# Decay exponents of a gated delta-rule kernel: one product of 72 rows from logs summed once, in place of two products with operands made on GpSimd

## The chip, the cores and the metric

The kernel runs on one core of one Trainium2 chip. The metric is the device time in microseconds (us) of one execution. Engines are called as in the profile: PE (TensorE) with its weight loads PEld, DVE (VectorE), ACT (ScalarE), POOL (GpSimd), SP (SyncE, which issues all DMAs here).

## The reference

One block of a transformer: AdaLN modulation, a gated delta-rule attention, then a feed-forward layer with 2:4 sparsity of the hidden activations. Eight sequences of 256 tokens with 256 channels; 16 key heads of 128, two value heads each, so 32 gates. What matters here is the attention:

```python
beta  = sigmoid(x @ W_b.T)                       # (B, T, 32)
dt    = softplus(x @ W_a.T + dt_bias)
decay = exp(-dt * exp(A_log))                    # (B, T, 32)
# per token t, head h, value head p:
Sk = k_t . S;  dv = b_t * (v_t - Sk);  S = S * d_t + outer(k_t, dv);  o = q_t . S
```

The log of the decay, g = -dt * exp(A_log), is what the change is about. In the chunked form of the recurrence each chunk of 128 tokens needs a 128 x 128 matrix of exp(sum of g from token i+1 to token j).

## The kernel before

The tokens are cut into chunks of 128. A step is one key head and two sequences, that is four chunks with two value heads each: U = 8 units of 128 x 128. There are 16 heads times 4 pairs of sequences, 64 steps. They run as a software pipeline, four deep: a body i works on step i (s0: projection, convolution, norms, decays, key products), step i-1 (s1: queries, values, first levels of the triangular inverse, z gate), step i-2 (s2: last levels, residue, state and outputs) and step i-3 (s3: output gate and projection). Each engine has its own list of the parts, written out in `body`, and runs it in that order; the engines meet at semaphores (`need(engine, name, count)`). There is a setup before the first body, two drain bodies (`last_bodies`) after the last, and then the feed-forward layer.

In the setup DVE makes `glog` (128 tokens x 16 chunks x 32 gates) and splits it into two f16 halves, `g_cols`. PE sums the logs along the tokens with the triangles `le`, `lt` and `gt` (three f32 products of 512 columns), and ACT takes the exponentials of these sums for the columns `cols`. For each head `head_columns` copies the head's part to `hg` and `hc`.

In each step POOL makes `g_le` (`decay_operand`, L378): for both halves the mask `le16` times the head's logs, 128 x 1024 f16. PE multiplies it by the mask `gt16` (`decay_product`, two halves h of four units, each half two products of 128x512 that add up in a PSUM bank). ACT then takes the exponentials (`decay_exp`), POOL multiplies by the masked beta (`decay_beta`), DVE by the key products.

The convolution over the tokens has four taps. PE projects block i (keys, queries, two values) into a bank, ACT writes the last tap (`last_tap`, L1096), DVE adds the three others (`convolve`, L1531); the bank is free for projection i+2 when all are done (`bank_project`). The state part of a step goes: PE `first_values`, ACT four scaled copies `us` (in `first_kept`, L1182), PE `state`. SP issues the loads of the next head's weights (`load_weights`, L270), which waits until both halves of the previous ones are made; ACT and DVE split one quarter of them in each step (`split_weights`).

The functions that the diff touches, with line numbers:

Of the kernel before, what the change touches and what calls it, by code (L numbers as in the profile page):

```python
# [35 lines left out]
GUARD = 0.25  # L36
W_SCALE = 64.0
# [8 lines left out]
def adaln_deltanet_ffn(nc, x, wh, nw, wba, dtb, alog, wgate, wup, wdown, cT, wmod, out):  # L46
    with ExitStack() as ctx:  # L47
# [26 lines left out]
        le16 = sb("le16", [P, P], F16)  # L74
        gt16 = sb("gt16", [P, P], F16)
# [11 lines left out]
        g_cols = sb("g_cols", [P, 2, NT, NV], F16)  # L87
# [7 lines left out]
        hg = sb("hg", [P, 2, 2, NT, PV], F16)  # L95
# [11 lines left out]
        g_le = sb("g_le", [P, 2, U, P], F16)  # L107
# [57 lines left out]
        same = hm  # L165
        gate_store = nc.dram_tensor("gate_store", (B, 2 * C), F32, kind="Internal").ap()
# [8 lines left out]
        wu_flat = [g_le[:].rearrange("p r u s -> p (r u s)"), yl[:, 0:2].rearrange("p l u s -> p (l u s)")]  # L175
# [47 lines left out]
        def all_steps(eng, body, last_bodies):  # L223
            for i in range(STEPS + 1):
                body(*lags(i))
            for i in range(STEPS + 1, STEPS + MOST):
                last_bodies(*lags(i)[2:])
# [23 lines left out]
        def _(sp):  # L251
# [13 lines left out]

            def load_weights(head, count):
# [5 lines left out]
            for head in range(1, NK):  # L272
                load_weights(head, head)
# [5 lines left out]
            sp.wait_ge(sig("gate_dma"), 16)  # L279
# [39 lines left out]
        def _(pool):  # L319
# [28 lines left out]
            triangle(le16, ones, ALU.is_ge, 0.0, 1, -1)  # L348
            triangle(gt16, ones, ALU.is_gt, 0.0, -1, 1)
# [22 lines left out]
            def decay_operand(s):  # L372
                n = N(s)
                need(pool, "hc", (head(s) + 1) * 2)
                need(pool, "e_ps", n * 2)
                ts = slice(blk(s) * TL, blk(s) * TL + TL)
                for part in range(2):
                    gp.tensor_tensor(g_le[:, part], le16[:].unsqueeze(1).broadcast_to([P, U, P]),  # L378
                                     hg[:, par(s), part, ts].rearrange("p t v -> p (t v)").unsqueeze(2)
                                     .broadcast_to([P, U, P]), ALU.mult).then_inc(sig("g_le"), 1)  # L380
# [7 lines left out]
            def masked_beta(s):  # L388

                n = N(s)  # L390
                need(pool, "hc", (head(s) + 1) * 2)
# [80 lines left out]
            def body(s0, s1, s2, s3):  # L472
                if s3:
                    gate_output(s3)
                if s1:
                    first_inverse(s1)
                if s0:
                    decay_operand(s0)
# [3 lines left out]
                if s1:  # L482
                    low_half(s1)
# [5 lines left out]
            def last_bodies(s2, s3):  # L489

# [4 lines left out]
                else:  # L495
# [9 lines left out]
                else:  # L505
# [17 lines left out]
        def _(pe):  # L523
# [52 lines left out]
            pe.wait_ge(sig("g_log"), 1)  # L576
            pe.wait_ge(sig("same_ready"), NL)
            pe.wait_ge(sig("pool_const"), 13)
# [7 lines left out]
            pe.wait_ge(sig("cum_exp"), 1)  # L586
            pe.wait_ge(sig("ba_copied"), 2)

# [15 lines left out]
            def decay_product(h, s):  # L604
                need(pe, "g_le", N(s) * 2 + 2)
                us_ = slice(4 * h, 4 * h + 4)
                for part in range(2):
                    ins = m(bP[h][:], gt16[:], flat(g_le[:, part, us_]), start=(part == 0), stop=(part == 1))
                ins.then_inc(sig("e_ps"), 1)
# [213 lines left out]
            def body(s0, s1, s2, s3):  # L823
# [3 lines left out]
                if s2:  # L827
                    level_right(4, s2)
# [3 lines left out]
                if s2:  # L832
                    level_rows(5, s2)
# [3 lines left out]
                if s2:  # L837
                    level_left(5, s2)
# [3 lines left out]
                if s2:  # L842
                    level_right(5, s2)
# [16 lines left out]
                if s2:  # L860
                    first_values(s2)
                if s1:
                    level_rows(0, s1)
                if s0:
                    need(pe, "iv", N(s0) * 2)
# [1069 lines left out]
```

## Time and profile before

| what | value |
|---|---|
| median of 3 runs | 2161.03 us (2156.39 to 2161.54) |
| the profiled execution's own time | 2155.69 us |
| its span | 2153.9 us, mean granted clock 0.986 |
| PE / PEld busy | 2068.8 us (96%) / 1709.5 us (79%) |
| DVE busy | 1890.6 us (88%) |
| ACT busy | 1599.1 us (74%) |
| POOL busy | 1317.9 us (61%) |
| DMA | 33.90 MB, 16 GB/s on average |

Busy time of an engine is the time in which at least one of its instructions runs. A matmul's duration holds its way through the array, which overlaps with the next one, so PE's pace is read from the starts. Idle time in front of an instruction carries the name of what ended it.

### The profile page before, as it was taken

The page shows a single profiled execution, that of the slowest core. Times are in us where ns is not written, and L with a number is a line of the kernel's source. Part 1 is how long each engine was busy: PE and PEld are TensorE (multiplying, and loading weights), DVE is VectorE, ACT ScalarE, POOL GpSimd, SP SyncE. Part 2 cuts the span into 40 slices and gives each one's busy share as a digit, 9 for nine tenths or more (in the row PEclk, how much of TensorE's full clock was granted, in tenths as well). Part 3 has the DMA queues.
Part 4 walks back from the last instruction along what each step waited for, and adds up shares of the span by engine and source line. Part 5 has one row for each costly group of instructions (what it writes and reads, how often), then busy time and mean ns, then how long its engine had stood idle before and what let it go on. Part 6 is the DMA issues. An engine that isn't in the chain of part 4 may idle for free. (4 is left out here: it accounts for less than half of the span.)

```text
span 2153.9 us, 59276 instructions
## 1 busy us (share of the span) xinstructions
PE 2068.8 (96%) x22950; PEld 1709.5 (79%) x22950; DVE 1890.6 (88%) x3119; ACT 1599.1 (74%) x3275; POOL 1317.9 (61%) x832
## 2 busy tenths in 40 slices
PE   5599999999999999999999999999999999997898
PEld 4378888888888888888888888888888888886787
DVE  5689888899888898888898888898888998886898
ACT  3477788887778887878877878877888877776332
POOL 3456666666666666666666666666666666663452
PEclk7899999999999999999999999999999999999999
DMA  2000000000000000000000000000000000002000
GB/s 103 8 4 19 2 21 2 22 2 22 2 22 2 21 2 2 21 2 21 2 22 2 21 2 21 2 2 21 2 22 2 22 2 21 2 2 91 23 23 23
DMA packets 12392, 33.90 MB, mean 16 GB/s; under 512 B 1100, under 2 KB 9420, under 8 KB 9684
## 3 DMA queue, kind: packets, MB, share of 16 engines
q1 hardware_dynamic: 12116, 30.11, 4.0%
q8 instruction: 187, 3.06, 0.6%
q14 instruction: 89, 0.73, 0.1%
HBM read 27.99 MB, written 2.11 MB: 14 GB/s over the span
## 5 line engine op out<-in xcount | busy, mean ns | idle before, releaser
L1531 DVE SCALAR_TENSOR_TENSOR cc<-bank,wc,cc 128x510 f32<-128x510 f32 (+2 forms) x768 | 546.9, 739 | 20.7 <-ACT cc L1096 16.0
L527 PE MATMUL bank<-h,w 128*128 128x512 f16 (+1 forms) x1920 | 419.0, 359 | 9.6 <-DVE cc L1531 3.1
L1606 DVE TENSOR_TENSOR yl<-bank,mask 128x512 f16<-128x512 f32 x384 | 262.7, 684 | 63.9 <-PE bank L527 63.9
L527 PEld LDWEIGHTS bank<-h,w 128*128 128x128 f16 x1920 | 171.5, 98 | 149.6 <-DVE cc L1531 19.6
L1166 ACT ACTIVATE invT<-bank 128x512 f16<-128x512 f32 x384 | 235.6, 614 | 59.2 <-PE bank L527 59.2
L1162 ACT ACTIVATE inv<-bank 128x512 f16<-128x512 f32 x384 | 232.0, 604 | 59.4 <-PE bank L527 59.4
L1096 ACT ACTIVATE cc<-bank,wc 128x512 f32<-128x512 f32 x256 | 177.8, 695 | 129.1 <-PE bank L527 129.1
L378 POOL TENSOR_TENSOR g_le<-le,hg 128x1024 f16<-128x1024 f16 x128 | 239.7, 1893 | 23.4 <-DVE hc L1492 23.4
L404 POOL TENSOR_TENSOR e_b<-ae,b_le 128x1024 f32<-128x1024 f32 x64 | 151.5, 2367 | 158.7 <-ACT ae L1152 158.7
L446 POOL TENSOR_TENSOR invT<-maskT,a 128x1024 f16<-128x1024 f16 x64 | 136.0, 2126 | 161.6 <-DVE a L1589 161.6
L386 POOL TENSOR_TENSOR rn<-n2m,mhalf 128x4 f32<-128x4 f32 x64 | 64.8, 1013 | 276.2 <-DVE n2m L1546 276.2
L527 PE MATMUL bank<-inv,a 128*128 128x64 f16 (+1 forms) x3584 | 218.0, 197 | 3.2 <-ACT inv L1162 2.2
L527 PEld LDWEIGHTS bank<-inv,a 128*128 128x128 f16 x3584 | 188.9, 98 | 17.9 <-ACT inv L1162 2.9
L412 POOL TENSOR_TENSOR osq<-o,zg 128x1024 f32<-128x1024 f32 x64 | 151.4, 2366 | 75.3 <-DVE oss L1643 75.3
L527 PE MATMUL bank<-w,goT 128*128 128x256 f16 x1536 | 188.3, 273 | 2.1 <-DVE goT L1656 2.1
L527 PE MATMUL bank<-w,h 128*128 128x256 f16 x1536 | 189.3, 273 | 0.0
L527 PEld LDWEIGHTS bank<-yl,invT 128*128 128x128 f16 x3072 | 132.8, 98 | 52.0 <-DVE yl L1606 39.4
L527 PE MATMUL bank<-yl,invT 128*128 128x64 f16 x3072 | 153.8, 193 | 10.1 <-DVE yl L1606 10.1
L527 PEld LDWEIGHTS bank<-w,goT 128*128 128x128 f16 x1536 | 146.0, 98 | 17.7 <-DVE goT L1656 2.3
L1228 ACT ACTIVATE zth<-bank 128x512 f32<-128x512 f32 x128 | 76.1, 594 | 108.0 <-PE bank L527 108.0
L527 PE MATMUL bank<-invT,yl 128*128 128x64 f16 x3072 | 153.9, 193 | 1.9 <-DVE yl L1606 1.1
L527 PEld LDWEIGHTS bank<-w,h 128*128 128x128 f16 x1536 | 141.8, 98 | 14.9
(212 smaller groups left out, 5297.1 us busy)
## 6 DMA issues: line engine op xcount, KB each, us to landing
w_raw<-in_wh SPq DMA_DIRECT2D x16, 1032.0 KB, 4.8
v<-in_x SPq DMA_DIRECT2D x4, 512.0 KB, 3.8
out<-sol SPq DMA_DIRECT2D x16, 128.0 KB, 1.7
w_raw<-in_wgate SPq DMA_DIRECT2D x1, 1024.0 KB, 4.7
cc<-in_wup SPq DMA_DIRECT2D x1, 1024.0 KB, 4.7
pt<-gate_store SPq DMA_DIRECT2D x2, 512.0 KB, 4.3
ae<-in_wdown SPq DMA_DIRECT2D x1, 1024.0 KB, 6.7
sol<-gate_store SPq DMA_DIRECT2D x2, 512.0 KB, 5.8
```

The source lines that it names most:

```text
L378: gp.tensor_tensor(g_le[:, part], le16[:].unsqueeze(1).broadcast_to([P, U, P]), hg[:, par(s), part, ts].rearrange("p t v -> p (t v)").unsq ...
L386: gp.tensor_tensor(rn[:], n2m[:, blk(s), 0], mhalf[:, 0:TL], ALU.pow).then_inc(sig("rn"), 1)
L404: gp.tensor_tensor(e_b[:, :, 1:P + 1], e_raw, b_le[:], ALU.mult).then_inc(sig("eb"), 1)
L412: gp.tensor_tensor(flat(osq[:]), o[:].rearrange("p t v d -> p (t v d)"), flat(zg[:]), ALU.mult).then_inc(sig("zo"), 1)
L446: gp.tensor_tensor(invT[:, ring(s)], maskT1[:].unsqueeze(1).broadcast_to([P, U, P]), a1[:, ring(s)], ALU.mult).then_inc(sig("it"), 1)
L527: return mm(o_, l_, r_, start=start, stop=stop, skip_group_check=True)
L1096: A(cc[:, i], bP[i % 2][:], ACT.Copy, scale=wc[:, par(s), i, 3:4]).then_inc(sig("tap"), 1)
L1162: A(lefts(inv[:, ring(s)], l), halves(bL[0], l), ACT.Copy).then_inc(sig("x_ready"), 1)
L1166: A(rights(invT[:, ring(s)], l), halves(bL[1], l), ACT.Copy).then_inc(sig("xt_ready"), 1)
L1228: A(zth[:, 2 * h:2 * h + 2].rearrange("p t d -> p (t d)"), bP[h][:], ACT.Tanh, scale=0.5 / W_SCALE).then_inc(sig("z_tanh"), 1)
L1531: V.scalar_tensor_tensor(dst, src, wc[:, par(s), i, 3 - j:4 - j], dst, ALU.mult, ALU.add).then_inc(sig(f"conv{i}"), 1)
L1606: V.tensor_tensor(lefts(yl[:, l], l), halves(bL[0], l), left(mask[:, l + 1, :], l).unsqueeze(1).broadcast_to([P, U, HP // n_, n_]), ALU.mu ...
```

## The change

The exponents come from one product with 72 rows (64 + 8) in place of 128 rows twice. In the setup the logs are clamped at -80 and cut into a coarse part on a grid and a fine rest. PE sums both along the tokens of each chunk, with the logs as weights, so that the sums lie as rows. ACT and DVE cut each sum into two f16 parts, which gives four rows per unit (`rank_parts`). One DMA writes them to `rank_store` in DRAM. For each step two DMAs (`load_rank`) bring the four rows of the eight units to every second of the rows 64 to 71 of `moving` and `standing`; the other four rows there hold -1 and 1. The rows 0 to 63 of both are constants made once on POOL, which put -60000 where the exponential has to be zero. `decay_operand`, `g_le`, `hg`, `g_cols`, `le16` and `gt16` go. The first loads of `rank_store` stand ahead of the weights of head 1 in SP's list. The lists of PE, ACT, DVE and POOL are in another order in several places, and ACT's `first_kept` is in two parts.

```diff
+        log_part = sol[:, 3].rearrange("p (t h) -> p t h", h=NV)
+        rank_parts = inv[:].rearrange("p r u s -> p (r u s)").rearrange("p (b k s) -> p b k s", b=NB, k=RANK)
+        rank_store = nc.dram_tensor("rank_store", (P, NB, RANK, P), F16, kind="Internal").ap()
+        def rank_rows(r, side):
+            return (moving, standing)[side][HP:HP + 2 * RANK, r].rearrange("p u s -> p (u s)")
 @@ SP
+            sp.wait_ge(sig("beta_rank"), 3)
+            sp.dma_start(rank_store, rank_parts).then_inc(sig("gate_dma"), 16)
+            sp.wait_ge(sig("gate_dma"), 32)
+            sp.wait_ge(sig("pool_const"), 21)
+            def load_rank(n):
+                need(sp, "e_ps", (n - 1) * 2)
+                hp_, b_ = n // NB, n % NB
+                src = rank_store[8 * hp_:8 * hp_ + 8, b_].rearrange("u k s -> k u s")
+                for side in range(2):
+                    dst = rank_rows(n % 2, side)[side:2 * RANK:2].rearrange("k (u s) -> k u s", s=P)
+                    sp.dma_start(dst, src).then_inc(sig(f"rank_in_{n % 2}"), 16)
+            load_rank(0)
+            load_rank(1)
-            for head in range(1, NK):
-                load_weights(head, head)
+            load_weights(1, 1)
+            for n in range(2, STEPS):
+                load_rank(n)
+                if n % NB == 0 and n // NB + 1 < NK:
+                    load_weights(n // NB + 1, n // NB + 1)
 @@ POOL
-            def decay_operand(s):
...
+            gp.memset(moving[0:HP], LOG_NONE).then_inc(cst, 1)
+            gp.memset(standing[0:HP], 1.0).then_inc(cst, 1)
+            pool.wait_ge(cst, 13)
+            for rows_, op, base, step, mult in ((moving, ALU.is_ge, 0, 1, -2), (standing, ALU.is_ge, -2, 1, -2)):
+                for r in range(2):
+                    gp.affine_select(out=rows_[0:HP, r], in_=rows_[0:HP, r], compare_op=op, ...)
+            pool.wait_ge(cst, 17)
+            for r in range(2):
+                gp.affine_select(out=moving[0:HP, r], in_=moving[0:HP, r], compare_op=ALU.is_ge, ...)
+            gp.memset(moving[HP:HP + 2 * RANK], -1.0).then_inc(cst, 1)
+            gp.memset(standing[HP:HP + 2 * RANK], 1.0).then_inc(cst, 1)
 @@ POOL body
                 if s1:
+                    low_half(s1)
                     first_inverse(s1)
-                if s0:
-                    decay_operand(s0)
 @@ PE setup
+            pe.wait_ge(sig("g_log"), 3 + 2 * NB)
+            for i in range(2):
+                for b in range(NB):
+                    ins = m(bank[i][:, b * P:b * P + P], sol[:, 1 + i, b * P:b * P + P], le[:])
+                ins.then_inc(sig("cum_ps"), 1)
 @@ PE decay_product
-                need(pe, "g_le", N(s) * 2 + 2)
-                us_ = slice(4 * h, 4 * h + 4)
-                for part in range(2):
-                    ins = m(bP[h][:], gt16[:], flat(g_le[:, part, us_]), start=(part == 0), stop=(part == 1))
+                need(pe, f"rank_in_{n % 2}", (n // 2 + 1) * 32)
+                K_ = HP + 2 * RANK
+                for u in range(4 * h, 4 * h + 4):
+                    ins = m(bP[h][:, (u % 4) * P:(u % 4) * P + P], standing[0:K_, n % 2, u], moving[0:K_, n % 2, u])
 @@ PE body, after first_values
-                if s1:
-                    level_rows(0, s1)
-                if s0:
-                    need(pe, "iv", N(s0) * 2)
-                    turn_keys(s0)
-                    turn_queries(s0)
+                if s0:
+                    turn_queries(s0)
+                    turn_keys(s0)
+                if s1:
+                    level_rows(0, s1)
+                if s2:
+                    state(s2)
+                if s1:
+                    level_right(0, s1)
+                    level_left(0, s1)
                 if s3:
                     bank_turn_output(0, s0, s3)
                     turn_output(0, s3)
                 if s2:
-                    state(s2)
-                if s1:
-                    level_left(0, s1)
...
 @@ ACT setup
+            for i in range(2):
+                act.wait_ge(sig("cum_ps"), i + 2)
+                A(rank_parts[:, :, 2 * i], bank[i][:].rearrange("p (b s) -> p b s", s=P), ACT.Copy).then_inc(sig("logs_read"), 1)
             act.wait_ge(sig("cum_ps"), 1)
             for i, bk in enumerate((bank[3], bank[6], bank[7])):
                 ins = A(cols[:, EG + i], bk[:].rearrange("p (t h) -> p t h", h=NV), ACT.Exp)
 @@ ACT body
+                    high_half(s1)
                 if s2:
                     inverse_right(4, s2)
...
                 if s0:
                     last_tap(3, s0)
                 if s2:
+                    first_scaled(s2)
+                if s0:
+                    squares(0, s0)
+                    squares(1, s0)
+                if s2:
                     first_kept(s2)
 @@ DVE setup
+                V.tensor_scalar(glog, glog, LOG_LEAST, None, ALU.max).then_inc(sig("g_log"), 1)
+                V.tensor_scalar(log_part, glog, LOG_GRID, None, ALU.add).then_inc(sig("g_log"), 1)
+                for b in range(NB):
+                    V.tensor_scalar(log_coarse[:, b], five(log_part)[:, b], -LOG_GRID, None, ALU.add)
+                for b in range(NB):
+                    V.tensor_tensor(log_fine[:, b], five(glog)[:, b], log_coarse[:, b], ALU.subtract)
+                V.reciprocal(cols[:, BETA], ba_one).then_inc(sig("beta_rank"), 1)
+                for i in range(2):
+                    V.tensor_tensor(rank_parts[:, :, 2 * i + 1], bank[i][:]..., rank_parts[:, :, 2 * i], ALU.subtract)
 @@ DVE body
                 if s0:
                     convolve(0, 1, s0)
+                if s1:
+                    decayed_queries(s1)
+                if s2:
+                    level_rows(5, s2)
+                if s0:
                     convolve(0, 2, s0)
...
+                    squared_norms(0, s0)
+                    squared_norms(1, s0)
+                    guarded_norms(s0)
                     convolve(3, 2, s0)
```

## Rows read from the trace of the kernel before

**Rows 1.** Busy time by stretch: length, then each engine, granted clock, DMA. One step.
```profile
1045.35:1074.80 29.45, 29.36 (x342) 24.29 (x341) 26.42 (x43) 23.74 (x50) 19.23 (x12) 1.00 0.01 2
```
**Rows 2.** Groups by line and shape: busy us, mean ns, idle before. The old product's weight loads.
```profile
L527 PEld LDWEIGHTS bank<-g_le,gt 128*128 128x128 f16 x256 | 16.1, 97 | 3.6 <-DVE cc L1531 3.6
```
**Rows 3.** Timeline of PE in one step: start, length, instruction, count.
```profile
1052.67 1.46 PE L527 MATMUL bank<-h,w 128*128 128x512 f16 x6
...
1060.88 0.61 PE L527 MATMUL bank<-ident,a 128*128 128x128 f16 x8
1061.33 0.61 PE L527 MATMUL bank<-invT,hm 128*128 128x128 f16 x8
1062.02 1.47 PE L527 MATMUL bank<-h,w 128*128 128x512 f16 x6
1063.32 1.05 PE L527 MATMUL bank<-v,tt 128*128 128x128 f32 x8
1064.21 0.40 PE L527 MATMUL bank<-inv,a 128*128 128x64 f16 x8
...
1065.80 1.03 PE L527 MATMUL bank<-sol,kn 128*128 128x256 f32 x4
...
1070.60 0.60 PE L527 MATMUL bank<-g_le,gt 128*128 128x512 f16 x2
1071.03 1.13 PE L527 MATMUL bank<-sol,tt 128*128 128x128 f32 x8
...
1082.12 1.46 PE L527 MATMUL bank<-h,w 128*128 128x512 f16 x6
```
**Rows 4.** Timeline of DVE, same step: first and last of twelve operations without a gap.
```profile
1054.89 1.53 DVE L1531 SCALAR_TENSOR_TENSOR cc<-bank,wc,cc 128x510 f32<-128x510 f32 x2 [0.21 <-ACT cc L1096]
...
1061.22 1.40 DVE L1531 SCALAR_TENSOR_TENSOR cc<-bank,wc,cc 128x506 f32<-128x506 f32 x2
```
**Rows 5.** Timeline of ACT, same step: the four scaled copies.
```profile
1064.42 1.15 ACT L1182 ACTIVATE sol<-bank,hc 128x128 f32<-128x128 f32 x4 [0.20 <-PE bank L527]
```
**Rows 6.** Timeline of DVE, end of the setup.
```profile
58.15 3.34 DVE L1477 RECIPROCAL cols<-sol 128x512 f32<-128x512 f32 x1
...
64.19 0.43 DVE L1483 TENSOR_SCALAR cols<-cols 128x512 f32<-128x512 f32 x1 [1.69 <-ACT cols L1080]
...
65.35 0.22 DVE L1492 COPY hc<-cols 128x128 f32<-128x128 f32 x1
```
**Rows 7.** Timeline of PE, last setup product and first projections.
```profile
61.52 1.02 PE L527 MATMUL bank<-sol,gt 128*128 128x512 f32 x2
64.36 2.75 PE L527 MATMUL bank<-h,w 128*128 128x512 f16 x12 [1.82 <-issue]
```
**Rows 8.** Timeline of ACT, end of the setup and first body.
```profile
56.73 1.28 ACT L1080 ACT_TABLE_LOAD   x1
62.58 1.57 ACT L1080 ACTIVATE cols<-bank 128x512 f32<-128x512 f32 x3 [4.57 <-PE bank L527]
...
67.73 0.62 ACT L1110 ACTIVATE w<-w_raw 128x512 f16<-128x512 f32 x1
71.09 0.69 ACT L1096 ACTIVATE cc<-bank,wc 128x512 f32<-128x512 f32 x1 [2.74 <-PE bank L527]
```
**Rows 9.** Timeline of POOL in the setup.
```profile
1.17 0.74 POOL L326 MEMSET yl<- 128x768 f16 x1
...
2.24 1.52 POOL L337 TENSOR_SCALAR_AFFINE_SELECT yl<-yl 128x128 f16<-128x128 f16 x6
...
37.09 4.95 POOL L366 TENSOR_SCALAR_AFFINE_SELECT mask<-mask 128x128 f16<-128x128 f16 x7 [2.83 <-DVE mask L1432]
...
65.72 3.74 POOL L378 TENSOR_TENSOR g_le<-le,hg 128x1024 f16<-128x1024 f16 x2 [23.43 <-DVE hc L1492]
```
**Rows 10.** Weight loads: page's DMA issues, and the tile's issues (ns, first and last start).
```profile
w_raw<-in_wh SPq DMA_DIRECT2D x16, 1032.0 KB, 4.8
...
L270 SPq DMA_DIRECT2D w_raw<-in_wh x15: 327/328/328, 50.7 to 1691.4; - x15
```

More of the change, by code:

```diff
@@ L36 @@
 GUARD = 0.25
+LOG_LEAST, LOG_GRID, LOG_NONE = -80.0, 49152.0, -60000.0
+RANK = 4
 W_SCALE = 64.0
@@ L106, in adaln_deltanet_ffn @@
         v = sb("v", [P, 2, TL, PV, P])
-        g_le = sb("g_le", [P, 2, U, P], F16)
+        moving = sb("moving", [P, 2, U, P], F16)
+        standing = sb("standing", [P, 2, U, P], F16)
         ae = sb("ae", [P, 2, U, P])
@@ L390, in masked_beta @@
                 n = N(s)
-                need(pool, "hc", (head(s) + 1) * 2)
+                need(pool, "hc", head(s) + 1)
                 need(pool, "eb", n)
@@ L494, in last_bodies @@
                         add_input(j)
-                else:
+                if not s2:
                     hidden_low(2)
@@ L504, in last_bodies @@
                     hidden_low(1)
-                else:
+                if not s2:
                     add_input(TL)
@@ L604, in decay_product @@
             def decay_product(h, s):
[L605 to L608 removed]
+                n = N(s)
+                need(pe, f"rank_in_{n % 2}", (n // 2 + 1) * 32)
+                K_ = HP + 2 * RANK
+                for u in range(4 * h, 4 * h + 4):
+                    ins = m(bP[h][:, (u % 4) * P:(u % 4) * P + P], standing[0:K_, n % 2, u], moving[0:K_, n % 2, u])
                 ins.then_inc(sig("e_ps"), 1)
@@ L1296, in body @@
                     values_turned(0, s1)
-                    high_half(s1)
                 if s2:
@@ L1352, in body, with last_bodies @@
                     z_tanh(1, s1)
-            def last_bodies(s2, s3):
+            def last_bodies(s0, s1, s2, s3):
+                if not s2:
+                    gate_tanh(0)
                 if s2:
@@ L1783, in body @@
                     convolve(2, 2, s0)
+                    convolve(3, 1, s0)
                     convolve(2, 3, s0)
-                    convolve(3, 1, s0)
                 if s1:
@@ L1806, in body @@
                     split_weights(s0)
-                if s2:
-                    if s1 and not s0:
+                if s1:
+                    if not s0:
                         gate_weights_low(2)
                         gate_weights_low(3)
+                if s2:
                     second_output(s2)
@@ L1832, in body, with last_bodies @@
                             gated(j)
-            def last_bodies(s2, s3):
+            def last_bodies(s0, s1, s2, s3):
+                if not s2:
+                    silu(0)
+                    hidden_stats(TL)
+                    hidden_product(0)
                 if s2:
+                    level_rows(5, s2)
+                    correction(s2)
                     for j in range(TL):
                         hidden_stats(j)
-                    level_rows(5, s2)
-                    correction(s2)
                     for j in range(TL):
```

159 lines of the change are left out of this document (69 added, 90 removed).

## The prediction

> **What bounds the kernel now.** The reader starts with the stretches of one step, then goes to the timeline of TensorE. One step of the pipeline takes 29.45 us, and in it PE is busy 29.36 us at full granted clock, VectorE 26.42, ScalarE 23.74, GpSimd 19.23 [rows 1]. A busy PE is not yet a PE at its pace, since the durations overlap, so starts are compared instead: eight f16 products of 128 columns take 0.45 us from start to start (56 ns each), four f32 products of 128 columns 0.89 us, and two f16 products of 512 columns 0.43 us [rows 3]. Adding such start-to-start times over the whole step gives about 28.9 us. What is left, 0.57 us, are waits, and all of them lie between the first projection of a step (1052.67) and its last (1062.02): 9.35 us, of which the eight products ahead of the last projection show the largest, 0.69 us where the eight before them took 0.45, so 0.24 us of wait. In the other 20.1 us PE follows its own pace. So PE's instruction stream sets the step, with VectorE's convolutions holding it once or twice in the first third: the convolutions run without a gap from 1054.89 to 1061.9, and the last projection starts 0.1 us behind them [rows 3, 4].
>
> **The change, part by part.** All terms are per step, for about 62 full steps of 64, unless said.
>
> *The product.* Removed are four f16 products of 128x512 (2 x 0.43 = 0.86 us). Added are eight of 72 rows and 128 columns, each with its own weights. No row has 72 rows of weights; the nearest are the eight 128-row products with own weights at 0.45 us in all [rows 3]. Bounds: 0.43 (columns alone) and 0.78 us, if each were paced by its weight load, 97 ns in the trace [rows 2]. I take 0.45, the row of the same form: -0.41 us, on PE's path.
>
> *The operands on GpSimd.* Two TENSOR_TENSOR go, 3.74 us together [rows 9]. GpSimd is idle a third of the step [rows 1] and its results were not late for PE, so this gives 0 by itself. low_half moves ahead of first_inverse, whose result is needed only at level 0, several us later. I cost the move at 0, since it lies beside PE's projections; without that cover I allow 0.3 us per step.
>
> *The DMAs.* Each step issues two loads of 8 KB on SP. A load for step n waits for the product of step n-2 and is used a step and more later, nearly 30 us after issue; a 1 MB load lands in 4.8 us [rows 10], so 0. In SP's queue load_weights(h+1) waits for the splits of step 4h-1, and load_rank(4h+1) behind it needs the product of that same step anyway, so nothing in the loop is queued up by it.
>
> *The order.* I laid the new order of PE, VectorE and ScalarE side by side with the durations of the rows.
> First third: project0, its tap on ScalarE, then VectorE does convolve(0,1) to convolve(1,3) with decayed queries, level rows and correction between them, the same set as before, only decayed queries earlier. Its sum from the end of the tap stays 7.0 us [rows 4], so the last projection still cannot start before 9.2 to 9.35 us after the first. I take 9.2: -0.15 us, between 0 and -0.57 if every wait went.
> Middle: state() now stands before the level-0 products instead of behind turn_output. It needs the four scaled copies on ScalarE. Before, the first values ran 1063.32 to 1064.21, the copies 1064.42 to 1065.57, and state() began at 1065.80 [rows 3, 5]. From the end of the first values to the end of the copies is 1.36 us. In the new order only the eight turns (0.91 us) and the level rows (0.24) lie between, 1.15 us: a new wait of 0.2 to 0.25 us. Bounds: 0 (copies earlier) and 0.9 us (a copy of the last tap or one other ScalarE operation of 0.6 to 0.7 slips in front). I take +0.25. ScalarE's squares now stand behind these copies.
> Rest: following each wait (kn, u1, ex, gw, x_ready, zg) I find 0.1 us or more to spare at all of them; high_half now stands in front of the right copy of level 4, and that copy comes 0.4 us before its reader. I cost these at 0, with -0.1 to +0.3.
> Sum per step: -0.41 - 0.15 + 0.25 = -0.31 to -0.33; 62 x -0.33 = -20.5 us.
>
> *The setup, once.* VectorE's glog ends at 58.15. Clamp and grid sum add 2 x 0.43 us, and eight small operations of 128 columns (0.22 each, overlapped 0.15) 1.2 us [rows 6]; the fine logs are there at 60.3, before PE is through the three cumulative products, which end at 62.54 and slip by 0.45 [rows 7]. Then eight f32 products of 128 columns, 1.8 us: 64.8. ScalarE copies the last at 65.5. The exponentials behind them take 1.57 us [rows 8]. Their table load (1.28 us) was hidden by the wait for PE, at 56.73; behind the copies it is not: 68.4, PE starts at 68.6 instead of 64.36. That is +4.2 us, +2.9 if the load stays early. VectorE: reciprocal until 63.5, two subtractions, one copy less for the head; it is not later than this.
> SP waits for the subtractions (66.2), stores 512 KB (about 4 us, by the 4.8 us of a double load [rows 10]), issues four small loads (0.33 us each) and only then the weights of head 1, before at 50.7 [rows 10], now near 72, landing at 77. ScalarE's split of these weights stands between tap 1 and tap 2. It was at 67.73 and tap 2 at 71.09 [rows 8]; with +4.2 the tap would be at 75.3, now 77.6: +2.3 us. About 1 us comes back, since tap 3 follows without its wait and the norms are taken before the last two convolutions. Sum of setup and first step: +5.5 us, between +2 and +9.
> GpSimd: it is free from 42.29 on [rows 9]. Added are four memsets of 2048 columns (0.74 us for 768, so 2.0 each) and six selects of 1024 columns (1.52 us for six of 128, so 2.0 each): 20 us, ready at 62.3, below 68.6. The mask selects took 0.71 each beside VectorE's work; at that pace the six last 34 us and end at 84.3, which would add 15.7 us. I keep 0.
> The Trainium skill (SBUF — State Buffer, Who interferes with whom) says that VectorE with two SBUF inputs and GpSimd reading SBUF hold each other up. The slow mask selects lie beside just such a VectorE operation (h minus its high half), the fast ones do not, so the trace agrees; here VectorE is mostly past such work when the new selects run.
>
> *Sum.* The profiled execution took 2155.69 us, its span 2153.9. 2155.7 - 20.5 + 5.5 = 2140.7. It lies 5.3 us under the median of the runs shown, 2161.03, at the low end of their 2156 to 2162; by the median the result is 2146. I give 2145.
>
> **Rivals.**
> A. *Waits of the first third vanish too and the state wait does not arise.* For it: the step's own pace is 28.9 - 0.41 = 28.5 us. Against it: VectorE's chain of 7.0 us has the same content. 62 x -0.95 + 5.5 = -53: about 2106.
> B. *The eight small products are paced by their weight loads.* At 97 ns each they save 0.08 instead of 0.41 us: 62 x 0.33 = +20, cancelling the gain: 2165, no change. Against it: the trace has 128-column products with their own weights at 56 ns.
> The Trainium skill (TensorE: Matmul & The Clock Gate, Back-to-back issue gap) gives 81 ns for a stream of load and matmul pairs of 128 columns. By it the eight would take 0.65 us, as an estimate, and the time would be 2157; the rows at 56 ns speak against it here.
> C. *The setup waits for GpSimd's selects.* +15.7 us: 2160, no change.
> D. *Slower: state() waits for its copies by a whole ScalarE operation and everything on PE behind it slides.* last_tap(3) is directly ahead of the copies, and the squares between them and u0. Every step loses x more than the 0.25 taken. The gain is gone at x = 15/62 = 0.24 us, one half of a copy. With x = 0.6: +37 - 15 = +22, so 2183. For it: my margins on ScalarE there are thin. Against: ScalarE waits 5.7 us per step elsewhere.
>
> **How the numbers follow.** A difference of 0.3%, 6.5 us, is about what a measurement here can tell from none. Chances: forecast 0.52 (2132 to 2155), A 0.14, B 0.07 and C 0.08 (no change), D 0.13, and 0.06 for a setup that costs more with a step that gives less, no change. Of the forecast's 0.52 some 0.05 falls within 0.3%. Faster 0.61, same 0.25, slower 0.14. The range reaches halfway to A and just past B: 2112 to 2170.
>
> **What would show it.** PE's first two-instruction groups of g_le gone, eight products of 128 columns in their place with starts 56 ns apart (B: near 97). Step period 29.1 us; last projection 9.2 us after the first. A wait of PE's weight loads on the scaled copies (sol, ScalarE) near 0.25 us per step; A has none, D has 0.8. First projection at 68 to 69 us with a table load before the exponentials; the weights of head 1 issued near 72. GpSimd busy about 15.4 us per step. The forecast is wrong if the period is over 29.4 or under 28.8, or the first projection is behind 75.

## The result and the profile after

The changed kernel took 2176.59 us (median of 4 runs, 2175.58 to 2178.15) against 2158.71 us of the kernel before on the same chip (its median with a fourth run added): a ratio of 1.0083, 95% interval 1.0065 to 1.0102. It is 0.8% slower. The forecast was 2145 in a range of 2112 to 2170. The profiled execution took 2175.58 us with a span of 2173.8, so 19.9 us more than the span of 2153.9 before.

Both traces can be cut at the same work. GpSimd's e_b product (the decay exponentials times beta) runs once per step, 64 times. Its row gives the first and the last start. Before:

```profile
L404 POOL TENSOR_TENSOR e_b<-ae,b_le x64: 2340/2368/2375, 81.4 to 1928.8; 128x1024 f32<-128x1024 f32 x64
```
After:
```profile
L435 POOL TENSOR_TENSOR e_b<-ae,b_le x64: 2352/2376/2377, 98.5 to 1940.7; 128x1024 f32<-128x1024 f32 x64
```

With the starts to two places the 19.9 us split into four parts. A period is the time from one start of e_b to the next.

| stretch | before | after | difference |
|---|---|---|---|
| start to first e_b | 81.42 | 98.50 | +17.1 |
| first three periods, pipeline filling | 80.46 | 82.47 | +2.0 |
| 60 full steps | 29.45 each | 29.33 each | -7.2 |
| last e_b to the end (drain, feed-forward) | 225.1 | 233.1 | +8.0 |

*The step.* The busy times in one step (length, then PE, PEld, DVE, ACT, POOL, granted clock, DMA) show GpSimd relieved as intended, 19.23 to 15.55 us, and a step that hardly moved:

```profile
1039.33:1068.65 29.32, 29.08 (x350) 24.48 (x347) 26.26 (x43) 24.00 (x49) 15.55 (x9) 1.00 0.01 3
```

The timeline of TensorE in the same step (start, duration, instruction) answers to [rows 3]:

```profile
1039.33 1.46 PE L554 MATMUL bank<-h,w 128*128 128x512 f16 x6
...
1048.63 1.47 PE L554 MATMUL bank<-h,w 128*128 128x512 f16 x6
1049.94 1.05 PE L554 MATMUL bank<-v,tt 128*128 128x128 f32 x8
1050.83 1.04 PE L557 MATMUL bank<-ident,cc 128*128 128x128 f32 x8
1051.70 0.40 PE L554 MATMUL bank<-inv,a 128*128 128x64 f16 x8
1052.23 1.13 PE L554 MATMUL bank<-sol,kn 128*128 128x256 f32 x4
1053.20 0.40 PE L554 MATMUL bank<-invT,yl 128*128 128x64 f16 x8
...
1058.97 0.39 PE L554 MATMUL bank<-moving,standing 72*128 72x128 f16 x4
1059.20 0.61 PE L557 MATMUL bank<-ident,kn 128*128 128x128 f32 x4
1059.64 0.39 PE L554 MATMUL bank<-moving,standing 72*128 72x128 f16 x4
1059.87 1.11 PE L554 MATMUL bank<-sol,pt 128*128 128x128 f32 x8
```

By starts, four 72-row products take 0.23 us (57 ns each), so the product fell from 0.86 to 0.46. The eight level rows ahead of state() (inv,a at 1051.70) take 0.53 from start to start instead of 0.24: a wait of 0.29. The state products (sol,kn) behind it take 0.97 instead of 0.86. The last projection starts 9.30 us after the first (before 9.35). Put together over one step: first third -0.05; from there to the end of query_state, with the level products left out of both sides since their number differs, +0.32; the stretch with the product -0.39; the rest, 7.84 us, is the same. Sum -0.12. The copies for which state() waits, answering to [rows 5], stand directly behind the last tap:

```profile
1050.14 0.69 ACT L1135 ACTIVATE cc<-bank,wc 128x512 f32<-128x512 f32 x1 [0.66 <-PE bank L554]
1051.03 1.15 ACT L1221 ACTIVATE sol<-bank,hc 128x128 f32<-128x128 f32 x4 [0.20 <-PE bank L554]
```

*The setup.* GpSimd makes the new constants while VectorE makes f16 copies. GpSimd after:

```profile
42.05 1.80 POOL L399 MEMSET moving<- 64x2048 f16 x1
43.79 1.80 POOL L400 MEMSET standing<- 64x2048 f16 x1
45.66 2.25 POOL L404 TENSOR_SCALAR_AFFINE_SELECT moving<-moving 64x1024 f16<-64x1024 f16 x2
...
54.45 2.02 POOL L411 MEMSET standing<- 8x2048 f16 x1
```
VectorE in the same stretch, after:
```profile
43.29 11.44 DVE L1483 COPY yl<-ident 128x768 f16<-128x768 f16 x8
54.65 2.10 DVE L1491 TENSOR_SCALAR kn<-v 8x512 f32<-8x512 f32 x1
```
and before, the same two operations:
```profile
43.48 2.23 DVE L1441 COPY yl<-ident 128x768 f16<-128x768 f16 x8
45.63 0.41 DVE L1449 TENSOR_SCALAR kn<-v 8x512 f32<-8x512 f32 x1
```

Eight copies grew from 2.23 to 11.44 us. These stand in front of the gates and the decay logs, and glog, which before ended at 58.2, ends at 68.9. TensorE and ScalarE behind it, answering to [rows 7, 8]:

```profile
69.45 2.07 PE L554 MATMUL bank<-sol,le 128*128 128x512 f32 x2 [26.15 <-DVE sol L1521]
...
74.73 1.98 PE L554 MATMUL bank<-le,sol 128*128 128x128 f32 x16
80.44 4.17 PE L554 MATMUL bank<-h,w 128*128 128x512 f16 x12 [3.73 <-ACT cols L1119]
```
```profile
76.75 0.60 ACT L1116 ACTIVATE inv<-bank 128x512 f16<-128x512 f32 x1 [0.30 <-PE bank L554]
77.37 1.28 ACT L1119 ACT_TABLE_LOAD   x1
78.66 1.57 ACT L1119 ACTIVATE cols<-bank 128x512 f32<-128x512 f32 x3
...
88.32 0.63 ACT L1149 ACTIVATE w<-w_raw 128x512 f16<-128x512 f32 x1 [2.99 <-DMA w_raw<-in_wh]
```

The 17.1 us of the setup come from these parts: 10.7 from glog, 0.5 from the clamp, 1.2 from the three cumulative products, 3.7 from their end to the first projection, and 1.0 from there to the first e_b. The cumulative products took 5.48 us at a granted clock of 0.51 where they took 4.26 at 0.66 before.

*The drain.* The 90 us behind the last e_b (length, PE, PEld, DVE, ACT, POOL busy, then the granted clock), before and after:

```profile
1928.76:2018.76 90.00, 68.97 (x751) 60.33 (x749) 61.40 (x106) 48.73 (x98) 39.72 (x39) 0.96 0.20 65
```
```profile
1940.70:2030.70 90.00, 71.59 (x706) 61.74 (x703) 54.39 (x91) 46.40 (x93) 37.21 (x35) 0.85 0.20 65
```

The clock is 0.85 instead of 0.96, and TensorE gets 706 instead of 751 products done. Single operations show the lower level, 1.2 GHz. The first state() behind the last e_b, before and after:

```profile
1948.99 1.13 PE L527 MATMUL bank<-sol,kn 128*128 128x256 f32 x4 [0.53 <-ACT sol L1182]
```
```profile
1961.17 2.07 PE L554 MATMUL bank<-sol,kn 128*128 128x256 f32 x4 [0.81 <-ACT sol L1221]
```

### The profile page after: what moved, and what is told of

It reads as the page before. It is cut to its first block and busy times, and to the rows that moved or that the text cites. A ratio compares the mean times of both kernels' runs of the same rounds, so it can differ in the third digit from the quotient of the medians.

```text
span 2173.8 us, 59888 instructions
## 1 busy us (share of the span) xinstructions
PE 2067.0 (95%) x23222; PEld 1734.5 (80%) x23222; DVE 1896.0 (87%) x3113; ACT 1616.9 (74%) x3277; POOL 1096.2 (50%) x712
## 5 line engine op out<-in xcount | busy, mean ns | idle before, releaser
L1584 DVE SCALAR_TENSOR_TENSOR cc<-bank,wc,cc 128x510 f32<-128x510 f32 (+2 forms) x768 | 536.2, 740 | 7.0 <-ACT cc L1135 4.5
L450 POOL TENSOR_TENSOR a_lo<-ae,a_hi 128x1024 f16<-128x1024 f32 x64 | 137.0, 2140 | 334.6 <-ACT a_hi L1197 334.6
L1205 ACT ACTIVATE invT<-bank 128x512 f16<-128x512 f32 x384 | 231.2, 602 | 99.9 <-PE bank L554 99.9
L554 PEld LDWEIGHTS bank<-inv,a 128*128 128x128 f16 x3584 | 182.6, 98 | 22.6 <-ACT inv L1201 18.2
L554 PEld LDWEIGHTS bank<-invT,yl 128*128 128x128 f16 x3072 | 134.8, 98 | 23.1 <-DVE yl L1659 3.0
L557 PE MATMUL bank<-ident,cc 128*128 128x128 f32 x1024 | 145.5, 275 | 1.1 <-DVE inv L1650 1.0
```

Source lines behind the costliest of these rows:

```text
L450: gp.tensor_tensor(a_lo[:, ring(s)], at, a_hi[:], ALU.subtract).then_inc(sig("al"), 1)
L554: return mm(o_, l_, r_, start=start, stop=stop, skip_group_check=True)
L557: return nc.tensor.transpose(o_, i_, id_)
L1205: A(rights(invT[:, ring(s)], l), halves(bL[1], l), ACT.Copy).then_inc(sig("xt_ready"), 1)
L1584: V.scalar_tensor_tensor(dst, src, wc[:, par(s), i, 3 - j:4 - j], dst, ALU.mult, ALU.add).then_inc(sig(f"conv{i}"), 1)
```

## Experiments

Each ratio is to runs of the kernel before on the same chip as the experiment. The step is the mean of 60 periods of e_b in the trace; e5, e6, e7 and e13 were run once.

**e1: the changed kernel with the lists of before.** On four engines:

```diff
-    body, last_bodies: the new order
+    body, last_bodies: the order of before (decay_operand left out)
```

> The changed kernel (72-row product, logs by DMA, new setup), with the lists of the four engines in the order of the kernel before. Theory T (three places: the setup costs about 18 us, the steady step gains only 0.12 us because the moved state() gives back what the product saves, the drain after the last full step costs 8 us by its order): the step is 29.45 - 0.40 = 29.05 us, and the drain is as before; the setup stays +16 to +18. Span of before + 17 - 61 x 0.40 = -7 us, so about 2146 to 2150, ratio 0.996 to 0.998. Rival R1 (the small products or the DMAs themselves cost the gain, the order is innocent): step stays 29.3, time about 2168, and a wait for rank_in or a slower product shows. Rival R2 (the tail is longer because of the colder clock from the step's new memory operands, not the order): the stretch from the last decay product to the end stays 8 us longer than before.

Measured: 2176.82 us, ratio 1.0087 (1.0073 to 1.0101). The forecast of 2146 to 2150 was missed, and so was each rival. The drain is back at 224.9 us with a clock of 0.96 over its first 90 us, and 1.2 of the 2.0 us of the filling are back. But the step is 29.445 us, the step of before to the hundredth: with these lists a product of half the time gives nothing. The first e_b comes at 100.2, so nearly all of the 19.1 us that the span is longer than before lie in the setup.

The drain is less fixed than these two traces say. The ten traces that drain with the lists of before (four of them with the moves of e9) took 224.8 to 229.7 us; the five with the new lists and an undivided state() took 233.1 to 235.1. In e6, whose drain does the same work as the kernel before, it took 229.7 at a clock of 0.95 over the whole drain, where before had 225.1 at 0.98. So the new order costs something there: 3.4 us between its shortest drain and the longest of the old lists, 8 us between the two kernels compared.

**e2: GpSimd's constants made earlier,** in the waits of the layer norm.

```diff
-            gp.memset(moving[0:HP], LOG_NONE) ...   # behind the mask selects
             def layernorm_rstd(b):
...
+                if b == 0:
+                    gp.affine_select(out=rows_[0:HP, r], ...)
```

> The changed kernel with GpSimd's ten constant operations (memsets and selects of moving and standing) moved from behind the level masks into GpSimd's waits for the layer norm statistics; same work, nothing else changed. Theory T: they held VectorE's eight copies of yl (11.44 us instead of 2.23) and the first of the gate rows (2.10 instead of 0.41) by the shared port, 10.9 us on the path; with the collision gone the first projection starts near 70 instead of 80.4 us and the time falls by 8 to 11 us, to about 2166 to 2168. Rival: the copies are slow for another reason (the different addresses of yl in SBUF), then they stay at 11 us and the time at 2176. A part could be lost again by new collisions with the layer norm's operations: up to 3 us.

Measured: 2170.34 us, ratio 1.0057 (1.0045 to 1.0070); first e_b at 91.9 instead of 98.5. The time is 2 us above the 2166 to 2168 expected, the eight copies take 2.23 us again, and the rival (slow copies because of their addresses) is out. But the constants now lie beside another operation of VectorE:

```profile
13.51 4.45 DVE L1462 TENSOR_SCALAR go<-o,knT 128x256 f32<-128x256 f32 x4 [1.45 <-POOL knT L387]
...
23.18 1.38 DVE L1462 TENSOR_SCALAR tt<-osq,knT 128x256 f32<-128x256 f32 x4 [1.42 <-POOL knT L387]
...
27.69 4.50 DVE L1462 TENSOR_SCALAR go<-zth,knT 128x256 f32<-128x256 f32 x4 [1.40 <-POOL knT L387]
```

The first and the third have GpSimd's constants beside them and take 4.5 us, the second does not and takes 1.38. The first has selects beside it and the third only MEMSETs. Of the 10.9 us expected back some 4 stayed away; the two slow operations together take 6.2 us more than at the pace of the fast one.

**e3: the new order with the old product,** in the kernel before.

> The kernel before, with its old product and GpSimd operands, but the four engines' lists in the new order (the decay operands stay ahead of the output scale on GpSimd). Theory T: the order costs +0.29 us per step (state() waits for its copies, the first third gives 0.1 back) and 8 us in the drain: step 29.73, time 2156 + 61 x 0.28 + 8 = 2181. Rival R1 (order innocent): step 29.45, drain as before, time 2156 to 2160.

Measured: 2279.08 us, ratio 1.0561 (1.0547 to 1.0576), step 31.26 us, far above the 2181 expected, so this run does not price the order by itself. In the new order low_half comes before the old operands on GpSimd, these (3.7 us) lie ahead of the output's scaling, and TensorE waits for that:

```profile
1004.36 0.63 PE L528 MATMUL bank<-ident,go 128*128 128x128 f32 x4 [1.43 <-POOL go L438]
```

With the old operands in this place the new order costs 1.81 us per step; other places for them were not tried.

**e4: only state() moved back** behind turn_output(0) in the changed kernel's list of TensorE.

> The changed kernel with one entry of PE's list moved back: state() behind turn_output(0) again, as before; all else as changed. Theory T: the wait of 0.29 us before state() and its slow start (0.97 instead of 0.86 us) go, 0.3 to 0.4 us per step: step 28.95 to 29.05, time 2176.6 - 61 x 0.35 = 2155. Rival (the wait only moves to the next reader, key_state or ScalarE's list, which was built for the early state): step stays 29.2 to 29.33, time over 2168.

Measured: 2249.27 us, ratio 1.0422 (1.0408 to 1.0436), step 30.51. The theory fell. The rival had the direction, a wait that moves to the next reader, but not the size: it gave a step of 29.2 to 29.33. ScalarE's list was written for the early state(); its copy of the state stands in front of what follows and now waits:

```profile
1031.31 0.60 ACT L1232 ACTIVATE sol<-bank 128x512 f32<-128x512 f32 x1 [1.43 <-PE bank L554]
```

**e5: the kernel before without the low half of the product.**

```diff
-                for part in range(2):
-                    ins = m(bP[h][:], gt16[:], flat(g_le[:, part, us_]), start=(part == 0), stop=(part == 1))
+                ins = m(bP[h][:], gt16[:], flat(g_le[:, 0, us_]))
```

> The kernel before, with the low half of the decay product left out (two products of 128x512 per step instead of four; the exponents lack the low part). It takes 0.43 us per step off PE and nothing else. Theory C (chains): in the old lists the two halves of the product stand in front of second_values, turn_normed and second_output, and these wait for VectorE's rest (rr), ScalarE's kn and u1, whose engines run without a gap for 8 us before; so PE's time there is not on the loop: step 29.4 to 29.45 us, and PE's waits for sol and kn grow by the 0.4 us. Theory P (PE bounds the step, as I predicted): step 29.02 us, time 27 us less.

Measured: 2159.16 us, step 29.445. As in e1, 0.4 us of products gone and none of it in the step.

**e6 and e7: VectorE's tap (3,1) and ScalarE's squares cut short,** in the kernel before and in e1. Both leave out part of the key and query norms and of one value block.

```diff
-                A(sq[:, i], grid(bB[i]), ACT.Square)
+                A(sq[:, i, :, 0:w_], grid(bB[i])[:, :, 0:w_], ACT.Square)   # w_ = 32 of 128 after step 0
-                dst = ...[:, :, j:T]
+                dst = ...[:, :, j:j + w_]                                   # w_ = 32 for (3, 1)
```

> The kernel before with shorter chains on the two other engines: ScalarE's two squares take only a quarter of the columns after the first step (about -0.3 us each), VectorE's first added tap of the second value block only 32 tokens of each sequence (about -0.5 us); the norms and one value block are wrong by it. PE's work is unchanged, with the product of 0.86 us. Theory C: step falls by the little that PE has left there, 0 to 0.15 us, to 29.3 to 29.45. Theory P: 29.45.

> The same two shortenings on the changed kernel with the old lists (e1), whose step was 29.445 with the product of 72 rows; the norms and one value block are wrong by them. Theory C: the chains were all that held it, so now the product's 0.4 us come out: step 29.0 to 29.1, that is 0.3 to 0.4 under the same shortenings with the old product. Rival (the product of 72 rows is slow on PE in these lists, or the small DMAs disturb): step stays above 29.35.

Measured: 2159.23 and 2173.8 us, steps 29.44 and 29.445, where e7 was expected at 29.0 to 29.1. No step moved, but the wait did. In e1 it is in front of second_values (1031.27 to 1031.68 us, where the product needs 0.22):

```profile
1031.27 0.39 PE L556 MATMUL bank<-moving,standing 72*128 72x128 f16 x4
1031.68 1.16 PE L556 MATMUL bank<-sol,tt 128*128 128x128 f32 x8
...
1033.15 0.39 PE L556 MATMUL bank<-moving,standing 72*128 72x128 f16 x4
1033.47 0.66 PE L559 MATMUL bank<-ident,kn 128*128 128x128 f32 x4
```

In e7 second_values follows at once, and the wait stands in front of turn_normed, for ScalarE:

```profile
1059.65 0.39 PE L556 MATMUL bank<-moving,standing 72*128 72x128 f16 x4
1059.88 1.11 PE L556 MATMUL bank<-sol,tt 128*128 128x128 f32 x8
...
1061.31 0.39 PE L556 MATMUL bank<-moving,standing 72*128 72x128 f16 x4
1061.85 0.66 PE L559 MATMUL bank<-ident,kn 128*128 128x128 f32 x4 [0.15 <-ACT kn L1168]
```

The reading that e9 and e13 test is that two chains end in these 2.9 us at the moment where the old product ended: VectorE's output_low and second_rest, and ScalarE's query_part, keys_normed and second_kept.

**e8: state() in halves.** In the changed kernel the products of sequence 0 wait for two scaled copies only.

```diff
-                need(pe, "us", N(s) * 4 + 4)
                 for g in range(BG):
+                    need(pe, "us", N(s) * 4 + 2 * g + 2)
```

> The changed kernel with one wait split: state() takes its first sequence when two of the four scaled copies are there, the second when all are. Theory T: PE's wait of 0.29 us and the slow first product (0.97 instead of 0.86) go, step 28.95 to 29.05, 61 x 0.3 = 18 to 20 us less than 2176.6, about 2157. Theory C in the new lists too (ScalarE's list from the copies to u1 runs without a gap and is what bounds): u1's copy now waits 0.20 us for PE, so at most about 0.2 us comes out: step 29.1 to 29.2, time 2163 to 2168.

Measured: 2163.53 us, ratio 1.0022 (1.0013 to 1.0030), step 29.19. The wait in front of state() is gone: level rows and state() now follow at 0.24 us. The products of state() themselves now take 1.10 us from start to start instead of 0.97, since those of sequence 1 wait for the other two copies; that is why only 0.14 of the 0.29 us come out, near the 29.1 to 29.2 of its second theory. The drain fell to 227.5 us as well.

**e9 and e10: both chains freed,** on e1 and on the kernel before.

```diff
 ACT
+                    keys_normed(s0)
                 if s2:
                     query_part(s2)
-                    keys_normed(s0)
                     second_kept(s2)
 DVE
+                    second_rest(s2)
                     output_low(0, s3)
-                    second_rest(s2)
 PE
-                    decay_product(0, s0)
                     second_values(s2)
                     level_left(1, s1)
                     level_right(1, s1)
+                    decay_product(0, s0)
```

> The changed kernel with the lists of before (as e1), and in them three moves: ScalarE's keys_normed ahead of query_part (it needed nothing of query_part, and second_kept behind it is what second_output waits for), VectorE's second_rest ahead of output_low(0), and TensorE's decay_product(0), which needs output_low(0), from ahead of second_values to behind level_right(1). Theory: in e1 and e5 the 0.42 us that the product gave back per step lie as waits in the 2.9 us between query_state and second_output: 0.19 in front of second_values (VectorE has output_low and then second_rest to do), 0.17 in front of turn_normed and second_output (ScalarE has 1.01 + 1.00 + 0.48 to do); both chains end where the old product ended, so freeing one alone (e7) gives nothing. With both freed the step falls from 29.445 by 0.3 to 0.4, to 29.05 to 29.15, and the time from e1's 2176.8 by about 62 x 0.35 = 22, to 2155 (2150 to 2160). Rival: VectorE is the bound of the loop as a whole (its busy time with the cost of its waits for buffers), then the waits turn up in another third and the step stays within 0.1 of 29.445, the time within 6 us of e1's.

> The same three moves on the kernel before, with its own product of 2 x 0.43 us. Theory: there TensorE has no wait in this stretch (product, second_values and turn_normed stand back to back), so the moves free nothing: step 29.40 to 29.45, time within 4 us of before (ratio 0.998 to 1.001). Rival (the lists of before were simply improvable, whatever the product): the step falls by 0.3 here as well, the time by about 20 us, and the change would have had no part in it.

Measured: e9 2173.47 us, ratio 1.0072 (1.0058 to 1.0085), step 29.32; e10 2163.45 us, ratio 1.0036 (1.0021 to 1.0050), step 29.55. The size was missed (29.05 to 29.15 and 2155 were expected of e9). The moves by themselves cost 0.10 us (e10): the product no longer covers VectorE's level_rows(1), for which TensorE waits 0.13 us in front of level_left(1). With the moves in both, the new product gives 0.23 of its 0.40. TensorE in e9:

```profile
1027.92 1.14 PE L556 MATMUL bank<-sol,tt 128*128 128x128 f32 x8
1029.02 0.41 PE L556 MATMUL bank<-yl,invT 128*128 128x64 f16 x8
1029.27 0.40 PE L556 MATMUL bank<-invT,yl 128*128 128x64 f16 x8
1029.51 0.61 PE L556 MATMUL bank<-moving,standing 72*128 72x128 f16 x8
1029.95 0.60 PE L559 MATMUL bank<-ident,kn 128*128 128x128 f32 x4
1030.47 1.16 PE L556 MATMUL bank<-sol,pt 128*128 128x128 f32 x8
```

second_values takes 1.10 from start to start where 0.97 is its pace, turn_normed 0.52 where it is 0.44.

**e13: e9 with the short tap and squares of e7.**

> The kernel of e9 with VectorE's conv tap (3,1) over 32 of 127 tokens and ScalarE's squares after the first step over a quarter of their elements (this part of the computation is left out). Together they take 0.4 to 0.5 us of work from VectorE and 0.7 from ScalarE, both ahead of second_rest. Theory: in e9 VectorE has no idle time between correction and split_weights and reaches second_rest, output_low(0) and level_rows(1) late, which is what TensorE still waits for (0.13 in front of level_left(1), 0.15 in front of second_output and turn_normed); with less to do the step falls from 29.32 to 29.05 to 29.15. The same cut on the old lists (e7) moved nothing, since ScalarE's keys_normed stood in the way there. Rival: TensorE's own order or its weight loads hold it, then the step stays at 29.3.

Measured: 2160.64 us, step 29.16, a hundredth outside the expectation. This kernel leaves out the same part of the computation as e7. The cut that gave nothing in e7 gives 0.16 us here, once ScalarE's chain is out of the way. From 29.445 the product's 0.40 would lead to 29.05; what is left above it, 0.11, is near the 0.13 that TensorE still waits in front of level_left(1) in this kernel. The rival, a bound on TensorE's side, is out for these 0.16 us, since TensorE's work is that of e9.

**e11: the setup mended.**

```diff
 POOL
+            gp.memset(moving[0:HP], LOG_NONE) ...          # before the layer norms
+                if b == 0: gp.affine_select(...) ...       # behind the first reciprocal root
 SP
+            load_weights(1, 1)
             sp.wait_ge(sig("beta_rank"), 3)
             sp.dma_start(rank_store, rank_parts)
 ACT
+            ins = A(cols[:, EG + i], ..., ACT.Exp)         # three, ahead of
             A(rank_parts[:, :, 2 * i], ..., ACT.Copy)
```

> The changed kernel with its setup mended in three places and nothing else: GpSimd's constants of the product (the memsets and selects) made at the start and in the first layer-norm wait instead of beside VectorE's copies of the decay logs' rows, SP's load of the next head's conv weights issued ahead of the rank loads, and ScalarE's exp ahead of its two rank copies. Theory: the 17.1 us by which the first step begins later are 10.7 of VectorE's copies held beside GpSimd's memsets, about 2.3 of SP's weights and 2 to 3 of the copies and the table load; so the first e_b comes at 82 to 87 us instead of 98.5, the steps stay at 29.33, the drain stays at 233, and the time is 2176.6 - 13 = about 2163 (2159 to 2166). Rival: the late start is TensorE's colder clock and the longer sums of logs themselves, then more than half of it stays and the time is above 2169.

Measured: 2164.88 us, ratio 1.0032 (1.0019 to 1.0045), first e_b at 85.8, step 29.33, drain 233.9. The first projection starts at 69.36. All as expected; the three mends were not run one by one.

**e12: the lists of e9 with the setup of e11.**

> The changed kernel with the lists of before and the three moves of e9, and the setup of e11. If both parts of the theory hold they add: from e1's 2176.8, 62 x 0.35 = 22 for the steps and 13 to 15 for the setup, 2140 (2134 to 2147), 0.9% below before. Rival: the step stays at 29.44, then 2162, no faster than before.

Measured: 2157.78 us, ratio 0.9998 (0.9989 to 1.0007), step 29.33, so the 2134 to 2147 expected were missed. The setup's gain added, and the part of the step's gain that e9 had missed was missing here too.

**e14: setup, halved state() and the old order in the drain,** on the new lists.

> The changed kernel with its own lists in the full steps, the setup of e11, state() in halves as e8, and the lists of before in the steps without a projection (the drain). Each was found by itself: setup -12.7 us of first e_b (e11), steps 29.19 instead of 29.33 (e8, its span 12.5 us shorter, its drain already 5.6 of them), drain 224.9 instead of e8's 227.5 (e1). If they add: e8's span 2161.3 - 12.7 - 2.6 = 2146, a time of about 2148 (2145 to 2152), 0.5% below before. Rival: the drain's lists meet other leftovers than in e1 and give nothing, then 2151; or the colder clock of TensorE takes part of it, then up to 2156.

Measured: 2149.13 us, ratio 0.9963 (0.9951 to 0.9975), within the 2145 to 2152 expected: 0.4% faster than before, step 29.19, first e_b at 87.2. The drain, in the profiled run 229.0 us at a clock of 0.95, was not the 224.9 expected. The times of this kernel lie in two groups, 2147.5 to 2149.9 and 2152.8 to 2153.0, with granted clocks of 0.982 and 0.978 over the span, and the profiled run is of the second. That the first group has the shorter drain was not traced.

## Why the prediction failed

The sum was -20.5 (steps) + 5.5 (setup) = -15; measured were -7.2 and +27.1, the latter being 17.1 of setup and 10.0 of filling and drain. The miss of 34.9 us is 13.3 in the steps, 11.6 in the setup and 10.0 in bodies that had no term. Point by point:

- **The product, -0.41 us per step: right in size** (0.86 to 0.46 us on TensorE, 57 ns each), **wrong in "on PE's path".** Rival B and the 81 ns of the Trainium skill (TensorE: Matmul & The Clock Gate, Back-to-back issue gap) are out for these products. What the step left out is on what the gain depends. With the old order the product only covered two chains of VectorE and ScalarE, and all of it turned into waits (e1, e5). The new order moves keys_normed ahead of query_part, as e9 does, and the stretch gives 0.39; that this move is what lets it through is argued from e9 and e13, no run takes it alone out of the new order. The prediction argued from TensorE's start-to-start times that it set this stretch; they cannot show that two others end at the same moment. The prediction gives no reason why the new order should let the product through, so that the changed kernel has this gain is luck.
- **The first third, -0.15: measured -0.05.** Its bound "9.2 to 9.35" held; I took the good end.
- **state() waits 0.25 us: the mechanism was right, the wait measured 0.29,** and the products behind it went from 0.86 to 0.97 us. Against that a neighbour gained 0.09 (sol,pt, 0.98 to 0.89), in all +0.32. e8 shows that 0.14 us of it can be had by waiting for two copies instead of four. Rival D was not it: a whole ScalarE operation did not slip in.
- **Sum per step -0.12, not -0.33**: 0.10 from the first third, 0.07 from state(), 0.02 from the product, and 0.02 because the forecast used -0.33 where its terms add up to -0.31. Over 60 steps some 12 us of the miss; the rest of its 13.3 is the count of 62.
- **The setup: +5.5, measured +17.1.** This step failed: no other term lies so far outside its own range (+2 to +9). The part behind the cumulative products was right: 3.8 us more expected from their end to the first projection, 3.7 measured, with the exposed table load; in e11, where the table load again runs while TensorE works, it is 2.0. Wrong was "VectorE is mostly past such work when the new selects run", and GpSimd "ready 62.3, I keep 0". GpSimd's work never was late (it was done at 56.5). It held VectorE's copies, 2.23 to 11.44 us, and the first operation of the gate rows, 0.41 to 2.10: 10.9 us. e2 and e11 show it by taking the overlap away. Another 1.2 us had no term: the cumulative products at the lower granted clock. I had quoted only one half of the Trainium skill's section (SBUF — State Buffer, Who interferes with whom), on operations with two inputs. The same section says that copies and scalar operations can enter VectorE's two-port modes, and that these contend with GpSimd for the length of a whole instruction. No trace shows the mode; what the trace shows agrees, 0.28 us each alone and 1.43 beside GpSimd.
- **The weights of head 1, +2.3 and 1 back:** expected issue near 72, which with the 10.7 us of glog and the 1.2 of the cumulative products is 84; the issue was at 83.5. The split at 88.32 waited 2.99 us for them, and from first projection to first e_b there is 1.0 us more than before, where 1.3 was expected. How much of it is theirs is open: in that stretch the twelve products of the first projection also took 4.17 us at a granted clock of 0.64, before 2.75 at 1.00.
- **The drain and the filling of the pipeline, not considered: +8.0 and +2.0.** The forecast multiplied the full step by 62 and had no term for bodies in which some stages are missing. There the order has other waits, and TensorE's granted clock is at its lower level for longer. e1 gives the 8.0 and 1.2 of the 2.0 back. How much of the 8.0 is the waits and how much the clock stays open.
- Rival C named the right culprit, the selects, with the wrong mechanism: TensorE was to wait for them, at +15.7. It was VectorE that they and the MEMSETs held, for 10.9. It had a chance of 0.08. (The chances as listed add up to 0.26 for the same and 0.13 for slower, where the prediction writes 0.25 and 0.14.)

## What to carry to other kernels

Work added "where the engine is free" must be checked against what its neighbours do at that time: here 14 us of work in GpSimd's idle time cost VectorE 11. Before an operation on the busiest engine is counted as a gain, ask what it covers: take it out of the kernel before (e5 is such a small edit) and see whether the step moves. A new order of a software pipeline has to be priced in its filling and draining bodies too, since they run with other waits and possibly at another clock.

## Unexpected in the hardware

- GpSimd MEMSETs, which read nothing, held VectorE as its selects did: the copies were slow throughout, and the run began beside two MEMSETs. In e2 four f32 TENSOR_SCALAR of 128x256 took 4.50 us instead of 1.38 beside MEMSETs alone, and 4.45 beside selects.
- The drain comes in few lengths. Over all traces it was 224.8 to 225.9, 227.5, 228.9 to 229.7 or 233.1 to 235.1 us, with a granted clock over the drain of 0.98, 0.97, 0.95 and 0.93. The kernel before and e6, whose drains do the same work, had 225.1 and 229.7. So a difference of 4 us there need not be work; what sets the clock there was not traced.
- State products of f32 directly behind a wait took 0.97 us where they take 0.86 without one.
